# The last two tiles' rows of unit 7 added by one-hot products on TensorE, with an earlier read-back and a reordered GpSimd norm

## What is computed

```python
x = x + xattn(layernorm(x), ctx, ctx)      # 16 heads, causal linear attention: elu + 1 on q and k,
                                           # running sums over k v, divided by the running sum of q
h = layernorm(x)
bids = sigmoid(h @ conf_w.T + conf_b) * wealth          # 8 experts
top_bids, chosen = top_k(bids, 2)
w = softmax(top_bids)
x = x + sum over the two chosen experts e of w_e * (silu(h @ gate_e.T) * (h @ up_e.T)) @ down_e.T
```

## Time and profile before

| | before |
|---|---|
| median of 3 runs | 331.06 us (330.39 to 331.72) |
| profiled execution, its own time | 329.64 us |
| its span, first to last instruction | 327.9 us |
| mean granted TensorE clock | 0.986 |
| busy share PE / DVE / ACT / POOL | 90% / 80% / 72% / 62% |

### The profile page before, as it was taken

How to read it: one execution, slowest core, us unless ns; L and a number is a source line. 1 busy time by engine, 2 the same in 40 slices (tenths; PEclk the granted TensorE clock), 3 DMA queues, 4 the chain that set the end, 5 groups by cost and what they waited for, 6 DMA issues and landing times.

```text
span 327.9 us, 12647 instructions
## 1 busy us (share of the span) xinstructions
PE 296.4 (90%) x4611; PEld 245.1 (75%) x4611; DVE 263.0 (80%) x721; ACT 234.5 (72%) x468; POOL 203.0 (62%) x304
## 2 busy tenths in 40 slices
PE   7888998997999999799599999999999899999970
PEld 5467685775768686676289989988999899899930
DVE  6699999998999999788777697989567566666763
ACT  3698896988798897957259777667667577677620
POOL 5672333687878789788567657877554345444530
PEclk9999999999999999999899999999999999999996
DMA  7231413333243422401264334587959657533895
GB/s 215 81 105 57 128 37 88 108 100 110 81 116 101 128 78 53 130 30 42 49 105 72 64 67 93 161 175 195 171 156 207 185 160 155 83 67 109 269 309 190
DMA packets 49034, 39.59 MB, mean 121 GB/s; under 512 B 32710, under 2 KB 39756, under 8 KB 48976
## 3 DMA queue, kind: packets, MB, share of 16 engines
q1 hardware_dynamic: 43648, 28.62, 34.6%
q0 software_dynamic: 4320, 8.47, 9.7%
q10 hardware_dynamic: 1008, 1.70, 1.5%
HBM read 15.29 MB, written 12.21 MB: 84 GB/s over the span
## 4 chain that ended last, share of the span: by engine, by line
PE 38%; DVE 24%; POOL 10%; issue 9%; SPq 7%; DMA 6%; ACT 5%; POOLq 0%; DVEq 0%; ACTq 0%
DVE Pm L1108 5%; POOL by_expert L644 4%; PE bank L1676 4%; PE scores L1678 3%; PE scores L1676 3%; PE bank L1677 3%; PE scores L1677 3%; PE bank L1678 3%; PE bank L1697 3%; PE bank L1698 3%; PE bank L1705 3%; DVE Vexp L1081 2%; SPq L541 2%; DVE w_both L1175 2%; DVE Z L1089 2%
## 5 line engine op out<-in xcount | busy, mean ns | idle before, releaser
L644 POOL DMA_INDIRECT by_expert<-token_rows,rows_to x64 | 68.3, 1067 | 22.2 <-issue 17.9
L772 POOL DMA_INDIRECT by_token<-y_sb,row_meta x55 | 56.8, 1032 | 40.6 <-ACT y_sb L960 29.3
L1377 DVE SCALAR_TENSOR_TENSOR hid<-scores,silu 128x512 f32<-128x512 f32 x71 | 48.0, 689 | 30.8 <-PE scores L1678 27.4
L976 ACT ACTIVATE hid_hi<-hid 128x512 f16<-128x512 f32 x71 | 44.2, 628 | 20.1 <-DVE hid L1377 19.3
L969 ACT ACTIVATE silu<-bank 128x512 f32<-128x512 f32 x71 | 42.0, 596 | 22.1 <-PE bank L1678 20.0
L1383 DVE TENSOR_TENSOR Kexp<-hid,hid_hi 128x512 f16<-128x512 f32 x71 | 47.8, 688 | 8.0 <-ACT hid_hi L976 4.2
L1697 PE MATMUL bank<-w_both,hid_hi 128*128 x248 | 34.7, 219 | 2.2 <-issue 2.2
L1508 PEld LDWEIGHTS scores<-qT,Kexp 32*128 32x128 f32 x1024 | 31.4, 186 | 6.7 <-issue 6.7
L1508 PE MATMUL scores<-qT,Kexp 32*128 32x128 f32 (+1 forms) x1024 | 35.8, 276 | 0.0
L1698 PE MATMUL bank<-w_both,hid_hi 128*128 x248 | 34.5, 219 | 0.0
L1108 DVE TENSOR_SCALAR Pm<-scores 128x768 f32<-128x768 f32 x32 | 30.5, 954 | 2.5 <-PE scores L1508 2.1
(11 more groups left out here) (405 smaller groups left out, 789.7 us busy)
## 6 DMA issues: line engine op xcount, KB each, us to landing
w_raw<-in_w_pack_dram SPq DMA_DIRECT2D x24, 256.0 KB, 2.7
x_all<-in_x_tok_dram SPq DMA_DIRECT2D x8, 256.0 KB, 2.8
cT<-in_ctx_t_dram SPq DMA_DIRECT2D x8, 256.0 KB, 3.1
w_raw<-w_both SPq DMA_DIRECT2D x2, 768.0 KB, 3.9
Pm<-w_both SPq DMA_DIRECT2D x2, 768.0 KB, 5.1
Vexp<-w_both SPq DMA_DIRECT2D x2, 768.0 KB, 3.8
single_more<-w_both SPq DMA_DIRECT2D x2, 768.0 KB, 5.3
out_dram<-x_all ACTq DMA_DIRECT2D x6, 256.0 KB, 3.3
```

The costliest lines, as they stand in the source:

```text
L644: pool.indirect_dma_start(by_expert, bass.IndirectOffsetOnAxis(ap=rows_to[u % 2][:, s, b:b + 1], axis=0), token_rows[u % 2][:, b, s, :], N ...
L772: pool.indirect_dma_start(by_token, bass.IndirectOffsetOnAxis(ap=number, axis=0), y_sb[:, k, s, :], None, bounds_check=NT * TOP - 1, oob_i ...
L1377: dve.scalar_tensor_tensor(hid[:, slot, :], bank[2 + slot], 1.0 / WSCALE, silu[:, slot, :], ALU.mult, ALU.mult).then_inc(hid_done, 1)
```

## The change

It does five things. (1) The last two tiles no longer write unit 7's rows to `by_token`: `bounds_check` for them ends where unit 7 starts. (2) These rows reach their tokens on TensorE: GpSimd writes the numbers 2t of unit 7's 512 tokens (`late_no`, an iota after tile 20's writes), VectorE turns the tiles' ids into token numbers (`late_numbers`, after tile 32) and compares them (`late_rows`, at tiles 33 and 34, giving one-hot matrices of 128x512), TensorE multiplies these with `y_sb` of tiles 38 and 39 (`late_sums`, eight products of 128x128x128 float32, between the sums of units 0 and 1), and VectorE adds the result to `x` before unit 6's adds (`add_late`). (3) The slots of `by_token` that thus stay unwritten are set to zero by one DMA of SyncE, ahead of the tile loads; GpSimd waits for it before tile 0's writes. (4) The read-back of unit 7 waits for the writes up to tile 37 and for tile 37's down products, and SyncE waits for all writes at its very end. VectorE's adds of units 2 and 3 move behind tile 39's passes. (5) In bodies 2 to 6, GpSimd's `tail(u - 1)` comes before `tail_rows(u - 2)`.

```diff
--- before.py
+++ after.py
@@ -155,6 +155,8 @@
         row_halves = [rows[:].rearrange("p b s r -> p (b s r)").bitcast(F16).rearrange("p (b s r) -> p b s r", b=UB, s=TOP) for rows in token_rows]
         row_ids = [rows[:].rearrange("p b s r -> p (b s r)").bitcast(U32).rearrange("p (b s r) -> p b s r", b=UB, s=TOP) for rows in token_rows]
         pad_row = sb("pad_row", [P, ROW])
+        late_pairs = sb("late_pairs", [P, LAST_SINGLES], U32)
+        late_ids = sb("late_ids", [P, LAST_SINGLES])
 
         full_u = sb("full_u", [1, E], U32)
         full = sb("full", [1, E])
@@ -243,6 +245,10 @@
 
         def back_of(flat):
             return flat.rearrange("p (b s d) -> p b s d", b=UB, s=TOP)
+
+        late_no = w_raw[0][:, 0, :]
+        late_hot = w_raw[0][:, 1:1 + LAST_SINGLES, :]
+        assert I == UT and LAST_SINGLES == 2
 
         y_back = ([back_of(cT_both[:].rearrange("p i c s -> p (i c s)")), back_of(expn[:].rearrange("p h t -> p (h t)")),
                    back_of(qT_both[:].rearrange("p i t -> p (i t)")), back_of(x2hat_both[:].rearrange("p i b d -> p (i b d)"))]
@@ -351,6 +357,12 @@
         y_loaded = [sem(f"y_loaded{i}") for i in range(UNITS - 1)]
         late_loaded = [sem(f"late_loaded{i}") for i in range(2)]
         late_sum = sem("late_sum")
+        late_ps = sem("late_ps")
+        late_base = sem("late_base")
+        late_no_made = sem("late_no_made")
+        late_ids_done = sem("late_ids_done")
+        late_hot_done = sem("late_hot_done")
+        cleared = sem("cleared")
         late_done = sem("late_done")
         sum_done = sem("sum_done")
         out_done = sem("out_done")
@@ -503,6 +515,10 @@
             pad_rows = pad_row[:].unsqueeze(1).to_broadcast([P, TB, ROW])
             sp.dma_start(by_expert[E * REGION:E * REGION + TT, :].rearrange("(s p) r -> p s r", s=TB), pad_rows).then_inc(padded, 16)
 
+            clear = zero_b[:].bitcast(F32)
+            own = by_token[(UNITS - 1) * UT * TOP:, :].rearrange("(p n) (h d) -> p (n h) d", p=P, d=P // 2)
+            sp.dma_start(own, clear.unsqueeze(1).to_broadcast([P, 2 * UB * TOP, P // 2])).then_inc(cleared, 16)
+
             def pad():
                 sp.wait_ge(pad_at_done, 1)
                 for e in range(E):
@@ -577,7 +593,8 @@
                     sp.dma_start(y_back[u], back[u]).then_inc(y_loaded[u], 16)
                     u = u + 1
             for k in range(4):
-                sp.wait_ge(y_stored[k], stored_by(TILES, k))
+                sp.wait_ge(y_stored[k], stored_by(TILES - LAST_SINGLES, k))
+            sp.wait_ge(y_ps, TILES - LAST_SINGLES)
             assert u == UNITS - 1
             for n in range(2):
                 part = slice(n * UB // 2, (n + 1) * UB // 2)
@@ -587,6 +604,8 @@
             sp.dma_start(out_tok[:, bass.ds(u * UB, UB), :], x_all[:, bass.ds(u * UB, UB), :]).then_inc(stored, 16)
             sp.wait_ge(late_done, 1)
             sp.dma_start(out_tok[:, HALVES[0], :], x_all[:, HALVES[0], :]).then_inc(stored, 16)
+            for k in range(4):
+                sp.wait_ge(y_stored[k], stored_by(TILES, k))
             sp.wait_ge(stored, 16 * (UNITS + 1))
 
 
@@ -652,12 +671,13 @@
                 pool.tensor_tensor(unit_start[:], unit_start[:], unit_ids[:], ALU.add).then_inc(id_next, 1)
 
             def body(u, par):
-                if u >= 2:
+                if last(u):
                     tail_rows(u - 2, par)
-                if last(u):
                     dispatch(u - 2, [0])
                 if not first(u):
                     tail(u - 1)
+                if u >= 2 and not last(u):
+                    tail_rows(u - 2, par)
                 if u == UNITS - 2:
                     dispatch(u - 2, range(UB))
                 elif u >= 2 and not last(u):
@@ -767,11 +787,17 @@
 
             def tile_step(i, k):
                 pool.wait_ge(y_done, blocks(i + 1))
+                if i == 0:
+                    pool.wait_ge(cleared, 16)
+                rows_there = NT * TOP if i < TILES - LAST_SINGLES else (UNITS - 1) * UT * TOP
                 for s in range(size(i)):
                     number = row_number[:, i % METAS, s, 1:2] if i < LAST else last_number[:, i - LAST, s, 1:2]
                     pool.indirect_dma_start(by_token, bass.IndirectOffsetOnAxis(ap=number, axis=0),
-                                            y_sb[:, k, s, :], None, bounds_check=NT * TOP - 1,
+                                            y_sb[:, k, s, :], None, bounds_check=rows_there - 1,
                                             oob_is_err=False).then_inc(y_stored[k], 16)
+                if i == FULL + 4:
+                    pool.iota(late_no, [[TOP, UT]], base=(UNITS - 1) * UT * TOP, channel_multiplier=0,
+                              allow_small_or_imprecise_dtypes=True).then_inc(late_no_made, 1)
                 if i == 3:
                     tail_ids(UNITS - 1, (UNITS - 1) % 2)
                 if 5 <= i < 5 + UB:
@@ -1411,11 +1437,36 @@
                     table_rows()
                 if i == 11:
                     table_columns()
+                if i == LAST + 1:
+                    late_numbers()
+                if LAST + 2 <= i < LAST + 2 + LAST_SINGLES:
+                    late_rows(i - LAST - 2)
                 if i == 13:
                     last_inside()
                 if i == 14:
                     last_waits()
 
+            def late_numbers():
+
+                for j in range(LAST_SINGLES):
+                    dve.wait_ge(last_loaded[LASTS - LAST_SINGLES + j], 32)
+                dve.tensor_scalar(late_pairs[:], last_number[:, LASTS - LAST_SINGLES:LASTS, 0, 1], 1, 1,
+                                  ALU.logical_shift_right, ALU.logical_shift_left).then_inc(late_ids_done, 1)
+                dve.wait_ge(late_ids_done, 1)
+                dve.tensor_copy(late_ids[:], late_pairs[:]).then_inc(late_ids_done, 1)
+
+            def late_rows(j):
+
+                dve.wait_ge(late_no_made, 1)
+                dve.wait_ge(late_ids_done, 2)
+                dve.tensor_tensor(late_hot[:, j, :], late_no, late_ids[:, j:j + 1].to_broadcast([P, UT]), ALU.is_equal).then_inc(late_hot_done, 1)
+
+            def add_late():
+
+                dve.wait_ge(late_ps, 1)
+                xu = x_all[:, (UNITS - 1) * UB:UNITS * UB, :]
+                dve.tensor_tensor(xu, bank[5].rearrange("p (b d) -> p b d", b=UB), xu, ALU.add).then_inc(late_base, 1)
+
             def add_first(u):
 
                 dve.wait_ge(y_loaded[u], 16)
@@ -1429,16 +1480,13 @@
                 xu = x_all[:, u * UB:(u + 1) * UB, :]
                 dve.tensor_tensor(xu, xu, y_back[u][:, :, 1, :], ALU.add).then_inc(out_done, 1)
 
-            for i in range(TILES - LAST_SINGLES):
-                tile_step(i, i % 4)
-            for i, u in zip(range(TILES - LAST_SINGLES, TILES), DVE_OUTS):
-                hidden(i, i % 4, 0)
-                add_first(u)
-                low(i, i % 4, 0)
-                add_second(u)
-            for u in DVE_OUTS[LAST_SINGLES:]:
+            tiles(dve, tile_step)
+            for u in DVE_OUTS:
+                if u == UNITS - 2:
+                    add_late()
                 add_first(u)
                 add_second(u)
+            dve.wait_ge(late_base, 1)
             for n, batches in enumerate(HALVES):
                 part = slice(n * UB // 2, (n + 1) * UB // 2)
                 dve.wait_ge(late_loaded[n], 16)
@@ -1744,8 +1792,21 @@
                 held_cols = tile_steps(i, TURN, held_cols, TURN if i + TURN < TILES else 0)
             down(TILES - 1, (TILES - 1) % 4, None)
 
+            def late_sums():
+
+                pe.wait_ge(late_hot_done, LAST_SINGLES)
+                for j in range(LAST_SINGLES):
+                    i = TILES - LAST_SINGLES + j
+                    pe.wait_ge(y_done, blocks(i + 1))
+                    for b in range(UB):
+                        ins = pe.matmul(bank[5][:, b * P:(b + 1) * P], late_hot[:, j, b * P:(b + 1) * P], y_sb[:, i % 4, 0, :],
+                                        start=(j == 0 and b == 0), stop=(j == LAST_SINGLES - 1), skip_group_check=True)
+                ins.then_inc(late_ps, 1)
+
             pe.wait_ge(silu_done, blocks(TILES))
             for u in (0, 1):
+                if u == 1:
+                    late_sums()
                 pe.wait_ge(y_loaded[u], 16)
                 xu = x_all[:, u * UB:(u + 1) * UB, :].rearrange("p b d -> p (b d)")
                 sums = bank[u].rearrange("p (b d) -> p b d", b=UB)
```

## The result

The changed kernel takes 338.13 us (median of 4 runs, 337.33 to 341.74), the kernel before 331.07 us beside it: ratio 1.0231, 95% interval 1.0181 to 1.0281. The prediction was 343.1 us: right in sign, the time inside the range, and the sum too long. The profiled execution took 337.46 us. Some executions run as a whole at a lower granted clock and are left out of the ratios (four of the seven of readback_waits_all, so its ratio says little); two profiled ones are among them, readback_waits_all (0.973) and adds_back_again (0.968), and of these only the end is compared, where the clock was at 1.00 up to 326 us.

The account below looks back on a forecast made before the run. VectorE was taken to pace the attention stage, TensorE the tiles from 31 on, and the read-back chain the end. Terms -3.5 + 4.4 + 1.7 + 9.4 = +12.0 on the 331.06 median gave 343.1 us, range 333.0 to 345.0.

Parts of the forecast that it names:

- Term two: VectorE at tile 32: waiting for tile 39's ids stalls TensorE ahead of tile 34, +4.4 us (3.9 to 4.8).
- Term three: TensorE behind the gap at tile 34: granted clock falls to half for 3.4 us, +1.7 us (0 to 1.7).
- Term four: Bodies 2 to 6: GpSimd's subtractions block VectorE's scans, and GpSimd idles in body 6, +9.4 us (0.2 to 9.5).
- the predicted 1.4: Body 6: GpSimd, free at 125.44, waits for the aggregates ending at 126.83, 1.4 us idle.
- rival (b): Bodies 2 to 6: both remaining scans go between the subtractions, 1.15 us lost a body, total 338.5 us, chance 0.22.
- The weight I gave `vdiff`: Attention bodies: scans taken to be blocked as `vdiff` was, by the whole pair of subtractions, 2.3 us a body.
- Term one: The end: unit 7's read-back goes 4.95 us sooner, VectorE's adds then finish last, -3.5 us (-1.5 to -4.0).
- Two waits of SyncE, so tile 37 had landed: The end: SyncE's waits were for tiles 38 and 39, so tile 37's writes landed by about 314.5; read-back at 314.6.
- Costed at nothing: SyncE's clearing write, GpSimd's iota at tile 20, VectorE's compares at tiles 33 and 34: covered by waits or idle time.

Follow-up runs that it names:

- readback_waits_all: order_and_ids with the read of unit 7 waiting for the writes of all 40 tiles again; ratio 0.9856 to the kernel before.
- adds_back: order_and_ids with VectorE's adds of units 2 and 3 back between the passes of tiles 38 and 39; ratio 0.9871, repeated 0.9956, to the kernel before.
- old_order: The changed kernel with GpSimd's earlier order in the bodies, rows ahead of the norm; ratio 1.0158 to the kernel before.
- gap_filled: The changed kernel with 14 unused identity products on TensorE ahead of its wait at tile 34; ratio 1.0102 to the kernel before.
- order_and_ids: The changed kernel with GpSimd's earlier order, ids' rounding at tile 35 and one-hot rows at 36 and 37; ratio 0.9916, repeated 1.0000, to the kernel before.
- before_adds_late: The kernel before with only the adds of units 2 and 3 moved behind tile 39's passes; ratio 0.9975 to the kernel before.
- adds_back_waits_all: adds_back with the read of unit 7 waiting for the writes of all 40 tiles; ratio 0.9967 to the kernel before.
- norm_first_alone: The kernel before with only GpSimd's new order, norm ahead of the rows; ratio 1.0084 to the kernel before.

## Why the prediction was right in sign and too long

**Term two, +4.4, measured 3.6.** The mechanism held as written. That it was smaller came from tile 0: TensorE was ready later, the ids were issued 2.8 us later (294.95 for 292.14). Without that lateness, in old_order, it was 6.0, as TensorE was ready at 289.2, ahead of its time in the earlier trace rows. The step that failed is taking 290.67 as fixed.

**Term three, +1.7, measured 1.7** (gap_filled).

**Term four, +9.4, measured +4.4 at tile 0.** This is the step that was mis-sized. The place was right: by the earlier trace rows the subtractions begin 1.75 us after the aggregates, and they begin 2.04 us after them (93.66 less 91.62). The difference is GpSimd's own `shift`, 0.44 us in place of 0.20, which itself lies under scans. By then three scans have gone, one is left, and it waits for one subtraction, not for both: 0.84 us a body in place of 2.3. In body 2, with two scans left, each waited for one subtraction: 1.84 us. From body 2's aggregates to body 6's VectorE so lost 3.2 us (75.13 for 71.90), where the prediction had 8.0. The prediction also put a gain at nothing that stood in the earlier trace rows: in the kernel before, the subtractions of body 2 lay over `before` (1.14 us) and over `place`:

```profile
47.90 0.89 DVE L1159 TENSOR_TENSOR place<-hot,rank 128x64 f32<-128x64 f32 x1
```

In the changed kernel these take 0.16 and 0.22 us, and body 2's aggregates end at 53.60 in place of 54.93. So body 6's aggregates end 1.9 us late (128.73 for 126.83). GpSimd used to begin its rows ahead of them and now waits for them: it starts at 128.82 in place of 125.44, 1.5 us more than the 1.9; this is the predicted 1.4. From there its own chain to tile 0's load takes 1.0 us longer, most of it where it waits for VectorE in turn (in body 6 the subtractions take 2.56 us for 2.29, the ids behind them 0.65 for 0.21), which I had also put at nothing. 1.9, 1.5 and 1.0 are the 4.4.

The one scan per subtraction is the turn-taking of rival (b), and its total, 338.5, is what came out; but that is luck: it was computed at 1.15 a body with nothing in body 3, its terms two and three are 1.4 us too long against the 4.7 of the tiles, and its end is 2.2 us too good, so errors cancel in it. The weight I gave `vdiff`, which had waited 2.4 us for both subtractions, was wrong for scans. What the Trainium skill says in SBUF — State Buffer, Who interferes with whom (two SBUF inputs on VectorE and a GpSimd instruction reading SBUF exclude each other for a whole instruction) fits all of it: scans 1.31 us, the weights' operation 1.02, the one-input stats untouched. By the same section the order of issue decides who waits; who goes next when both engines have an instruction ready it does not say, and there `vdiff` (it waited for both subtractions) and the scans (for one each) differ. The prediction called `vdiff` a case of this rule, but its record starts 0.31 us before the first subtraction's (156.72 and 157.03 in the earlier trace rows) and it was still the one that waited. Why stays open.

**Term one, -3.5, measured -1.3.** The read's start was late in the changed kernel, and where it did start on time (order_and_ids) it took 7.12 us. Both failures are the DMA engines: I had costed the collision of reads and stores at up to 2 us as a bound, and it was the rule. "Two waits of SyncE, so tile 37 had landed" was right for the kernel before and did not carry over, since its write now meets the read of unit 6. The same end took between 12.8 and 14.7 us in seven profiled executions, so a single -1.3 is no fine measure. They fall in two groups: 14.6, 14.6 and 14.7 where the ids' wait is moved, with unit 7's read right behind that of unit 6, 2.5 to 2.6 us after the last pass; 12.8 to 14.4 in the four with the wait at tile 32, where unit 6's read goes 0.4 to 0.5 us before that pass and unit 7's only at 3.8 to 5.4 us. The late products on TensorE, 1.7 us by my estimate, took 1.95 and were not on the path.

**Costed at nothing**: the clearing write, the iota and the compares. No kernel tested one of these alone; with the order and the ids set right (order_and_ids) the kernel is not slower than before, so together they cost no more than the new end gains.

**Version left.** order_and_ids with the adds back is 0.4% to 1.3% faster than the kernel before in its two measurements, of which the second, narrower interval is 0.9920 to 0.9992. That version is clearly ahead of the changed kernel; against the one before it is 1.5 us ahead by the narrower measurement and 4.3 by the wider, and the narrower just excludes no gain.

## What to carry to other kernels

Before a GpSimd operation is moved, list what VectorE runs at its new time, and count the operations with two inputs in SBUF that are still to come there: each can lose a whole GpSimd instruction (here 0.9 us of a subtraction of 1.2), those with one input lost nothing here. Count also what the operation held up at its old time. A wait put at the head of an in-order queue costs what is behind it, and if its data arrive at a fixed time, every gain made earlier runs into it. At the end of a kernel add up the bytes of reads and stores first: where the DMA engines are full, an earlier read is only a slower one.

## What the runs showed that I had not expected

The same code at the same place got a different clock. order_and_ids and its repetition from 79.8 to 86.6 us, in that order:

```profile
79.80:86.60 6.80, 6.80 (x102) 5.97 (x105) 5.28 (x23) 4.91 (x10) 5.49 (x8) 0.50 0.29 90
```

```profile
79.80:86.60 6.80, 6.79 (x180) 5.71 (x179) 6.53 (x30) 6.58 (x14) 5.50 (x7) 1.00 0.30 92
```

TensorE is busy throughout in both, and in both it had waited 1.5 us for ScalarE's `x2hat` a little before; one runs at half clock for 6.8 us and gets 102 products done, the other at full clock 180. That is why tile 0's load stands at 162.4 in one and 160.0 in the other. Single executions of one kernel lie apart by as much as the effects studied here (326.4 to 329.7 us in the five runs behind order_and_ids's first ratio), and such falls of the clock can be part of it.

The wait of 1.5 us belongs to the old order. It is there in the kernel before, old_order, before_adds_late, adds_back_waits_all and both executions of order_and_ids; in two of these six, the one above and adds_back_waits_all, the clock fell behind it. In the six profiled executions where TensorE waits 0.2 to 0.6 us at this place (the five with the norm first, and adds_back) it did not fall there. So the new order may give back in some executions a part of what it costs; this would fit norm_first_alone, which is only 2.8 us slower with its tile 0 5.0 us late, but no run tested it.
